# A two-layer conditioned network on one core: unread products in the first layer's TensorE pauses, the gates moved back, and the second layer's set-up with element 0's scores first

## The chip, the core and the metric

The kernel runs on one core of a Trainium2 chip. Its engines are TensorE (PE, matrix products; PEld are its weight loads), VectorE (DVE), ScalarE (ACT), GpSimd (POOL) and SyncE (SP, which here only issues transfers). The metric is the device time of one execution in microseconds (us).

## The reference

Input x is 2 batch elements of 512 tokens with 128 channels, and a condition vector of 128 per element. Two layers follow one another.

Layer 0 quantises weights to -1, 0, 1 and activations to 8 bits around every linear map:

```python
def _bitlinear(x, w, nw, b=None):
    xn = x * rsqrt(mean(x**2) + 1e-08) * nw
    xq = _act_quant(xn)            # round(xn * 127 / max|xn|), row by row
    return xq @ _weight_quant(w).T
# six parameters per element come from the condition by a small network
mx = _layernorm(x) * (1 + sc_msa) + s_msa
i, f, g = _bitlinear(mx, wi), sigmoid(_bitlinear(mx, wf)), _bitlinear(mx, wg)
o = scan over tokens: h = f * h + silu(i) * (1 - f)
x = x + g_msa * _bitlinear(_rmsnorm(o) * silu(g), wo)
x = x + g_mlp * gated MLP of (_layernorm(x) * (1 + sc_mlp) + s_mlp), 128 -> 2*512 -> 128
```

Layer 1 is plain float: `mod = silu(condition) @ Wada + bada` gives two shifts, two scales and two gates; then causal attention with 16 heads of 8 channels over 512 tokens, and a GELU MLP of 128 -> 512 -> 128, each added to x after it is multiplied by its gate.

## The kernel before

Tokens lie on the 128 partitions in 4 tiles (NT) per batch element b = 0, 1. The PSUM has 8 banks of 512 floats. Every engine has its own program, written out by hand in one order, and the engines meet only through semaphores. An instruction that waits holds all that stands behind it on its engine. There is no planner.

**Layer 0** (36 to 121 us of the profiled execution) is a chain that passes between the engines. For each element VectorE forms `mx` and three scaled copies `u3` (L1165 to L1182), GpSimd takes roots (`root`, L402), TensorE turns `u3` into columns by transposes (`to_columns`, L1538), ScalarE copies them to bf16 (`xq3`, L630), TensorE multiplies (`rows_product`, L1543), ScalarE makes sigmoids (`gate`, L648), VectorE the input of the scan, the scan itself (L1210) and the output rows. Then come the residual, the layer norm, and the MLP with its product `prod` (L1318), its scaled copy `uh` (L458), its quantisation (L1335), its columns (L1644) and its second product (L1653).

Between the pieces TensorE runs **unread products**: `idle_products(n, bk)` (L1549) issues n bf16 products of 128x512 into a bank whose content nobody reads. They stand in TensorE's order like any other instruction, each string after some wait and ahead of the next piece of work.

The **gates** of layer 1 (`layer_gates`, L1530 and L1532, four products of 128x128 and four one-row bias products, float32, into bank 7) stand after element 0's three products; ScalarE copies them to `gates` (L668) between two of its sigmoid groups, and GpSimd multiplies `Wproj`, `bproj`, `W2` and `b2` by them (L436 to L444) between the roots of stage 0 and stage 1.

**Layer 1's set-up** (119 to 147 us). `xhat` is transposed, ScalarE modulates it to `xmT` (L752), and `project_rows(b)` makes queries, keys (L1681, float32, banks 2 and 3) and values (L1687, bank 0). Queries and keys are each split in three bf16 parts: part 0 on ScalarE (L781), the rest on VectorE (L1359), part 1 on ScalarE (L789), part 2 on VectorE (L1365). The parts are stacked along the partitions in QS and KS. For element 0's first two head groups this is done by TensorE with `pick` (L1672) and copies (L768, L770, L1373); for the rest by DMAs that `stack_parts` issues, the queries on SP, the keys on GpSimd (L345, 12 per element).

Attention runs in **8 groups** n = 0 to 7 (element n // 4, four heads each). A group has 12 score items (`score_item`, L1732 to L1734, in three rotating banks); VectorE takes the negative row maximum of each (`row_maxima`, L1384). After the group's 12 items GpSimd splits the maxima in three bf16 parts (`split_maxima`, L484 to L490). TensorE transposes them after item 3 of the next group (`maxima`, L1744), ScalarE copies them (L821), SP writes them into three rows of QS (L379), and only then can the group's transposed scores, five `exp_slot`s (L1773 to L1779), begin, with the exponentials on ScalarE (L807) and the products with the values (L1793) behind them. In the kernel before TensorE's order of set-up is: element 0's projections, its picks, element 1's columns and all of its projections, then group 0. GpSimd's is: both elements' key stacks, the bias `bproj` added to xs (L476), then `split_maxima(0)`. The picks of the second group (PICK_AT) stand inside group 0.

## Time and profile before

| | |
|---|---|
| median of 3 runs | 238.95 us (237.7 to 239.03) |
| profiled execution, its own time | 238.84 us |
| its span, first to last instruction | 237.0 us |
| mean granted TensorE clock | 0.928 of full |
| busy: PE, PEld, DVE, ACT, POOL | 76%, 45%, 71%, 67%, 30% |
| chain that ended last, by engine | PE 38%, DVE 28%, ACT 14%, POOL 10%, issue 7%, DMA 1% |

The chain that ended last is followed back from the last instruction, at each step to what released it. A granted clock of 1.00 is 2.4 GHz and 0.50 is 1.2 GHz. Of the chain, the unread products of L1549 hold 5.3% of the span and the key stacks of L345 5.6%.

### The profile page before, as it was taken

Reading aid. Unit: us, or ns where it says so; the run is one execution under the profiler, and the core shown is the slowest. Engines: PE = TensorE matmul, PEld = TensorE weight load, DVE = VectorE, ACT = ScalarE, POOL = GpSimd, SP = SyncE. Lnnn points to the kernel's source line nnn. Section 1 sums busy time; section 2 is a strip of 40 time slices with the busy share of each in tenths; the row PEclk is TensorE's granted clock in tenths of the full one; section 3 lists DMA queues with packets and bytes.
Section 4 is the critical chain, followed back from the end, with each engine's and each line's share of the span. In section 5 each row is a group of like instructions: output and inputs, shape, how many; then the busy total and the mean of one; then the engine's idle time right before and its main releaser. Section 6 shows DMA issues by size and latency. Waiting matters only on the chain.

```text
span 237.0 us, 4518 instructions
## 1 busy us (share of the span) xinstructions
PE 180.2 (76%) x1640; PEld 107.6 (45%) x1644; DVE 169.1 (71%) x494; ACT 158.3 (67%) x346; POOL 71.3 (30%) x112
## 2 busy tenths in 40 slices
PE   0223369699575896559786986999999999889894
PEld 0202335676332343126453543765655665544763
DVE  3758779999688979897776694877977887342511
ACT  4798999676986866956137623765865775786141
POOL 8031231019222153971129990101110110130210
PEclk9999999776989799958999995699999999999999
DMA  5999100000000000000002340321000000000011
GB/s 140 410 427 362 52 0 0 3 1 0 0 1 0 3 0 0 1 0 0 3 1 93 97 81 23 48 53 22 3 5 2 5 3 5 2 3 0 0 47 44
DMA packets 4635, 11.50 MB, mean 49 GB/s; under 512 B 1283, under 2 KB 2788, under 8 KB 3974
## 3 DMA queue, kind: packets, MB, share of 16 engines
q1 hardware_dynamic: 3654, 10.03, 12.7%
q0 software_dynamic: 960, 1.19, 2.1%
q8 instruction: 13, 0.21, 0.4%
q14 instruction: 8, 0.07, 0.1%
HBM read 8.23 MB, written 0.52 MB: 37 GB/s over the span
## 4 chain that ended last, share of the span: by engine, by line
PE 38%; DVE 28%; ACT 14%; POOL 10%; issue 7%; DMA 1%; SPq 0%; DVEq 0%; ACTq 0%; POOLq 0%
DVE negmax L1384 7%; PE ps L1793 6%; POOL KS L345 6%; PE ps L1538 5%; PE ps L1549 5%; PE ps L1732 2%; ACT PT L807 2%; PE ps L1829 2%; DVE mx L1265 2%; PE ps L1773 2%; PE ps L1823 2%; DVE bnst L923 1%; ACT junk L623 1%; DVE amax L1308 1%; ACT xhat L594 1%
## 5 line engine op out<-in xcount | busy, mean ns | idle before, releaser
L1384 DVE TENSOR_REDUCE negmax<-ps 128x1 f32<-128x384 f32 (+3 forms) x96 | 51.2, 594 | 14.1 <-PE ps L1734 14.0
L807 ACT ACTIVATE PT<-ps 128x1024 f32<-128x1024 f32 x40 | 39.6, 1031 | 20.7 <-PE ps L1779 20.5
L1549 PE MATMUL ps<-k_b 128*128 128x512 bf16 x119 | 34.2, 449 | 6.6 <-DVE prod L1318 4.4
L1732 PE MATMUL ps<-KS,QS 48*128 48x128 bf16 (+3 forms) x128 | 32.2, 321 | 1.4 <-DVE negmax L1384 0.8
L1773 PE MATMUL ps<-QS,KS 51*128 51x512 bf16 (+3 forms) x128 | 24.9, 315 | 1.6 <-DMA QS<-nmT 1.6
L1549 PEld LDWEIGHTS ps<-k_b 128*128 128x128 bf16 x119 | 13.0, 113 | 24.7 <-issue 8.1
L1733 PE MATMUL ps<-k_b 64*128 64x128 bf16 x128 | 24.2, 229 | 0.0
L1734 PE MATMUL ps<-k_b 64*128 64x64 bf16 x128 | 21.7, 198 | 0.0
L402 POOL TENSOR_TENSOR rstd<-veps,mhalf 128x4 f32<-128x4 f32 x8 | 8.4, 1046 | 40.6 <-DVE veps L930 38.0
L1793 PE MATMUL ps<-PT,V 128*9 128x512 f32 (+3 forms) x256 | 20.4, 434 | 0.0
L402 POOL TENSOR_TENSOR rms<-vms,mhalf 128x4 f32<-128x4 f32 x10 | 10.8, 1079 | 27.5 <-DVE vms L1130 27.2
L1779 PE MATMUL ps<-k_b 64*128 64x128 bf16 x128 | 19.0, 225 | 0.0
L1776 PE MATMUL ps<-k_b 64*128 64x64 bf16 x128 | 17.9, 197 | 0.0
L484 POOL CAST nmpart<-negmax 128x16 bf16<-128x16 f32 x8 | 1.6, 199 | 52.9 <-DVE negmax L1384 52.9
L1732 PEld LDWEIGHTS ps<-KS,QS 48*128 48x128 bf16 x128 | 11.2, 96 | 10.5 <-DVE negmax L1384 7.9
L1734 PEld LDWEIGHTS ps<-k_b 64*128 64x128 bf16 x128 | 12.1, 103 | 4.4 <-issue 0.8
L345 POOL DMA_DIRECT2D KS<-part x24 | 13.4, 567 | 1.1 <-ACT part L781 0.6
L1733 PEld LDWEIGHTS ps<-k_b 64*128 64x128 bf16 x128 | 11.7, 101 | 0.0
L1773 PEld LDWEIGHTS ps<-QS,KS 51*128 51x128 bf16 x128 | 9.4, 97 | 3.7 <-issue 2.1
L1447 PE MATMUL ps<-k_f,cq 2*128 2x2 f32 x8 | 1.5, 252 | 11.6 <-DVE cq L965 11.6
L594 ACT ACTIVATE xhat<-xs,nbias,rstd 128x128 f32<-128x128 f32 x20 | 8.2, 480 | 3.1 <-DVE nbias L946 3.1
L1779 PEld LDWEIGHTS ps<-k_b 64*128 64x128 bf16 x128 | 9.2, 99 | 1.9 <-issue 0.5
(242 smaller groups left out, 452.4 us busy)
## 6 DMA issues: line engine op xcount, KB each, us to landing
w<-in_wa SPq DMA_DIRECT2D x2, 1152.0 KB, 9.4
lw<-in_l_w SPq DMA_DIRECT2D x1, 1280.0 KB
brow<-in_bcast_rows SPq DMA_DIRECT2D x1, 1152.0 KB, 15.4
mw<-in_main_w SPq DMA_DIRECT2D x1, 1024.0 KB, 12.5
KS<-part POOLq DMA_DIRECT2D x12, 64.0 KB, 3.4
QS<-part SPq DMA_DIRECT2D x12, 64.0 KB
cw<-in_cond_w SPq DMA_DIRECT2D x1, 576.0 KB, 4.0
xs<-in_x SPq DMA_DIRECT2D x1, 512.0 KB, 5.9
```

The source lines that it names most:

```text
L345: queue.dma_start(stack[first:first + HD, skip:, :], part[b][i][want][half * ROWS + skip * HD:(half + 1) * ROWS, :]).then_inc(done, 16)
L402: return nc.gpsimd.tensor_tensor(r, v, mhalf[0:v.shape[0], 0:v.shape[-1]], ALU.pow)
L807: nc.scalar.activation(PT[n % 2][:, s, :], bank(2 * (use % 2), 2), ACT.Exp).then_inc(S["p_ready"], 1)
L1384: V.tensor_reduce(negmax[n % 2][:, qt, h0:h0 + nh], bank(S_BANKS[k % 3])[:, 0:nh * w].rearrange("p (h w) -> p h w", w=w), AX.X, ALU.max, n ...
L1549: T.matmul(bank(bk).rearrange("p (r n) -> p r n", n=P), ident_b, ident_b.unsqueeze(1).to_broadcast([P, NT, P]), start=True, stop=True)
L1732: T.matmul(dst, QS[b][rows, h, tok(qt)], KS[b][rows, h, 0:w], start=True, stop=False)
L1733: T.matmul(dst[:, w - P:w], k_of("pickLo", r), k_of("maskQlo", r), start=False, stop=False)
L1734: ins = T.matmul(dst[:, w - P // 2:w], k_of("pickHi", r), k_of("maskQhi", r), start=False, stop=True)
L1773: T.matmul(dsts[half], KS[b][rows, h, tok(kt)], QS[b][rows, h, kt * P:L], start=True, stop=False)
L1776: T.matmul(dsts[half][:, 0:P // 2], k_of("pickLo", r), k_of("maskKlo", r), start=False, stop=False)
L1779: ins = T.matmul(dsts[half][:, 0:P], k_of("pickHi", r), k_of("maskKhi", r), start=False, stop=True)
L1793: ins = T.matmul(bank(PV_BANKS[n])[32 * j:32 * j + HD + 1, kt * P:L], V1[b][:, kt, g * HG + j, :], src, start=(kt == 0), stop=(kt == 2))
```

## The change

Unread products in layer 0: 11 become 19 ahead of element 0's first columns; 10 new after the shifts and 9 (were 8) after element 0's forget-gate columns; 8 new between the scanned rows of element 0 and the input columns of element 1; 3 new after each `output_columns`; at the MLP's end 16 new after the fifth product, 8 (were 10) after the last, 9 (were 6) after `uh`.

The gates: the products move from behind element 0's three products to behind `output_product(1)`, in place of 9 unread products; ScalarE's copy moves between `centre(0)` and `centre(1)`; GpSimd's eight multiplications move behind the roots of the MLP's end.

The set-up: element 1's `xhat` is made on GpSimd, not on ScalarE; element 1's projections move into groups 0 and 1 (one side after item 9, one after item 11, the values after the first item of group 1), and with them ScalarE's copies and VectorE's rests; GpSimd stacks element 0's keys, splits group 0's maxima, stacks element 1's keys, splits group 1's maxima, adds the bias.

```diff
-PICK_AT = (2, 4, 6, 8)
+PICK_AT = (3, 5, 7, 10)
+SIDE_AT = (9, 11)
@@ gpsimd
-                if stage == 0:
-                    pool.wait_ge(S["mod_copied"], 2)
-                    pool.wait_ge(S["m_q"], 4)
-                    for b in range(B):
...
             for stage in range(3, 5):
...
+            pool.wait_ge(S["mod_copied"], 2)
+            pool.wait_ge(S["m_q"], 4)
+            for b in range(B):
+                ga, gm = gates[:, 0, b, :], gates[:, 1, b, :]
+                nc.gpsimd.tensor_tensor(wproj_g[:, b, :], lw[:, slice(*LW["Wproj"])], ga, ALU.mult
+                                        ).then_inc(S["gated"], 1)
...
             pool.wait_ge(S["ln_root"], 3 * B)
+            for t in range(NT, B * NT):
+                ins = nc.gpsimd.tensor_scalar(xhat[:, t, :], xs[:, t, :], bnmv[:, t, 0:1], rstd[:, t:t + 1],
+                                              ALU.subtract, ALU.mult)
+            ins.then_inc(S["xhat_ready"], 1)
             for b in range(B):
                 nc.gpsimd.memset(V1[b][:, :, :, HD:HD + 1], 1.0).then_inc(S["v_ones"], 1)
-                pool.wait_ge(S["stack_init"], B)
-                stack_parts(pool, b, 1)
-            ...
-                nc.gpsimd.tensor_tensor(xs[:, tiles(b), :], xs[:, tiles(b), :], over_tiles(bproj_g[:, b, :]), ALU.add
+            pool.wait_ge(S["stack_init"], B)
+            stack_parts(pool, 0, 1)
             for n in range(N_GROUPS):
                 split_maxima(n)
+                if n == 0:
+                    stack_parts(pool, 1, 1)
+                if n == 1:
+                    pool.wait_ge(S["gated"], 4 * B)
+                    pool.wait_ge(S["xhat_ready"], B)
+                        nc.gpsimd.tensor_tensor(xs[:, tiles(b), :], xs[:, tiles(b), :], over_tiles(bproj_g[:, b, :]),
+                                                ALU.add).then_inc(S["biased"], 1)
@@ scalar
-            for b in range(B):
-                centre(b, B + b + 1, S["xhat_mid"])
+            centre(0, B + 1, S["xhat_mid"])
+            act.wait_ge(S["gate_pe"], 1)
+            nc.scalar.activation(gates[...], bank(7), ACT.Copy).then_inc(S["mod_copied"], 1)
+            centre(1, B + 2, S["xhat_mid"])
...
+            first_part(0, 0)
+            first_part(0, 1)
+            second_part(0, 0)
+            second_part(0, 1)
+            picked(0, 0, 0, 1, 4)
+            picked(0, 1, 0, 3, 6)
+            modulate_columns(1, 0)
+            value_rows(0)
+            picked_second(0)
+            picked_second(1)
+            picked_second(2)
+            first_part(1, 0)
+            picked_second(3)
+            first_part(1, 1)
+            value_rows(1)
...
                 copy_maxima(n - 1)
+                if n == 1:
+                    second_part(1, 0)
+                    second_part(1, 1)
@@ vector
-            ln_bias(1, 2 * B + 2)
-                    if n == 0 and i == 1:
-                        split_rest(1)
-                    if n == 0 and i == 5:
+                    if n == 0 and i == len(S_ITEMS) - 1:
+                        split_rest(1, (0,))
+                    if n == 1 and i == 1:
+                        split_rest(1, (1,))
+                    if n == 1 and i == 5:
                         split_last(1)
@@ tensor
-            idle_products(11, 2)
+            idle_products(19, 2)
...
                 if b == 0:
                     layer_shifts()
-                    layer_gates()
+                    pe.wait_ge(S["mx_ready"], 2)
+                    idle_products(10, 5)
                 pe.wait_ge(S["sig_ready"], 3 * b + 1)
                 to_columns(bank(4 * b + 2), lambda t: fg[b][:, 1, t, :], S["fT_pe"])
                 if b == 0:
-                    pe.wait_ge(S["mx_ready"], 2)
-                    idle_products(8, 5)
+                    idle_products(9, 5)
             scanned_rows(0)
+            idle_products(8, 4)
             input_columns(1)
             idle_products(8, 4)
...
             output_columns(0)
+            idle_products(3, 0)
             output_product(0)
             output_columns(1)
+            idle_products(3, 0)
             output_product(1)
-            idle_products(9, 1)
+            layer_gates()
             pe.wait_ge(S["ln_var"], B + 1)
...
+            pe.wait_ge(S["prod_ready"], B * 2 + 1)
+            idle_products(16, 0)
             pe.wait_ge(S["prod_ready"], B * NT)
-            idle_products(10, 0)
+            idle_products(8, 0)
             pe.wait_ge(S["uh_raw"], B * NT - 1)
-            idle_products(6, 0)
+            idle_products(9, 0)
...
-            project_rows(0)
+            project_side(0, 0)
+            project_side(0, 1)
+            project_values(0)
...
-            project_rows(1)
...
                     if n == 0 and i in PICK_AT:
...
+                        if v == 1:
+                            pe.wait_ge(S["xmT_ready"], B)
...
+                    if n == 0 and i in SIDE_AT:
+                        project_side(1, SIDE_AT.index(i))
+                    if n == 1 and i == 0:
+                        project_values(1)
```

## Rows read from the trace of the kernel before

**Rows 1.** Stretches of the span: busy time (instructions) by engine, granted clock, DMA share, GB/s.

```profile
47.00:50.40 3.40, 3.40 (x24) 2.70 (x21) 3.33 (x5) 3.08 (x16) 0.65 (x1) 1.00 0.00 0
50.40:57.20 6.80, 6.80 (x22) 4.14 (x22) 6.63 (x24) 3.60 (x12) 3.73 (x7) 0.50 0.00 1
...
101.60:108.40 6.80, 4.91 (x12) 1.79 (x13) 6.09 (x17) 3.76 (x10) 4.67 (x4) 0.50 0.00 0
...
142.60:152.80 10.20, 8.29 (x92) 5.70 (x92) 6.20 (x12) 5.88 (x6) 0.96 (x5) 0.50 0.26 41
173.60:182.10 8.50, 8.19 (x142) 5.17 (x137) 6.84 (x14) 5.87 (x7) 0.84 (x4) 1.00 0.01 3
```

**Rows 2.** The chain of waits, 36 to 60 us: start, duration, what.

```profile
43.32 2.75 PE ps L1538 x12
...
50.08 0.41 PE ps L1532 x2
...
52.99 3.41 PE ps L1549 x8
56.40 2.21 PE ps L1538 x16
```

**Rows 3.** VectorE in order of time, 36 to 74 us: start, duration, form, [idle before].

```profile
55.38 1.10 DVE L1198 SCALAR_TENSOR_TENSOR orow<-fg 128x512 f32<-128x512 f32 x1
...
61.37 1.13 DVE L1189 SCALAR_TENSOR_TENSOR fg<-ps,dq,fg 128x128 f32<-128x128 f32 x4 [1.44 <-ACT fg L648]
62.53 0.69 DVE L1198 SCALAR_TENSOR_TENSOR orow<-fg 128x512 f32<-128x512 f32 x1
```

**Rows 4.** TensorE in order of time, 36 to 74 us.

```profile
63.77 3.34 PE L1549 MATMUL ps<-k_b 128*128 128x512 bf16 x8
```

**Rows 5.** TensorE in order of time, 74 to 121 us.

```profile
78.32 9.53 PE L1549 MATMUL ps<-k_b 128*128 128x512 bf16 x37
88.10 2.76 PE L1549 MATMUL ps<-k_b 128*128 128x512 bf16 x12 [0.25 <-DVE mx L1125]
...
103.49 6.04 PE L1549 MATMUL ps<-k_b 128*128 128x512 bf16 x16 [4.39 <-DVE prod L1318]
...
112.75 1.05 PE L1653 MATMUL ps<-mwq,xh 128*128 128x128 bf16 x16 [0.60 <-DVE xh L1341]
```

**Rows 6.** VectorE in order of time, 74 to 121 us.

```profile
107.23 0.88 DVE L1335 TENSOR_SCALAR uh<-uh,minv 128x512 f32<-128x512 f32 x2
...
111.32 1.29 DVE L1341 TENSOR_SCALAR xh<-ps 128x512 bf16<-128x512 f32 x2 [1.54 <-PE ps L1644]
```

**Rows 7.** GpSimd by line and shape, whole span: busy, mean ns, idle before.

```profile
L440 POOL TENSOR_TENSOR w_g<-lw,gates 128x512 f32<-128x512 f32 x2 | 3.0, 1524 | 0.0
...
L407 POOL TENSOR_SCALAR cwq<-cw,whalf 128x768 bf16<-128x768 f32 x1 | 2.2, 2211 | 2.2 <-DVE cwq L1030 2.2
```

**Rows 8.** TensorE in order of time, 118 to 132 us.

```profile
126.56 1.34 PE L1672 MATMUL ps<-part,picks 128*128 128x512 bf16 x4 [1.73 <-ACT part L789]
...
129.21 1.98 PE L1681 MATMUL ps<-xmT,lw 128*128 128x512 f32 x4
131.03 1.05 PE L1687 MATMUL ps<-lw,xmT 128*128 128x128 f32 x8
```

**Rows 9.** ScalarE in order of time, 118 to 160 us.

```profile
124.34 1.65 ACT L594 ACTIVATE xhat<-xs,nbias,rstd 128x128 f32<-128x128 f32 x4 [0.62 <-DVE nbias L946]
```

**Rows 10.** VectorE in order of time, 118 to 160 us.

```profile
132.52 0.76 DVE L1384 TENSOR_REDUCE negmax<-ps 128x2 f32<-128x256 f32 x2 [2.23 <-PE ps L1734]
...
137.72 5.36 DVE L1384 TENSOR_REDUCE negmax<-ps 128x1 f32<-128x384 f32 x10
```

**Rows 11.** The chain of waits, 134 to 164 us.

```profile
139.23 2.49 POOL xs L476 x2
...
142.87 0.60 PE ps L1744 x4
...
144.89 1.89 DMA QS<-nmT
```

More of the change, by code:

```diff
@@ L711, in _ @@
             load_table(ACT.Silu, 1)
-            for b in range(B):
-                centre(b, B + b + 1, S["xhat_mid"])
+            centre(0, B + 1, S["xhat_mid"])
+            act.wait_ge(S["gate_pe"], 1)
+            nc.scalar.activation(gates[:, :, :, :].rearrange("p i b d -> p (i b d)"), bank(7), ACT.Copy
+                                 ).then_inc(S["mod_copied"], 1)
+            centre(1, B + 2, S["xhat_mid"])
             for b in range(B):
@@ L1352, in _, with split_rest @@
                     ln_apply(list(range(NT)), 2 * B + 1, S["xhat_ready"])
-            ln_bias(1, 2 * B + 2)
-            def split_rest(b):
-                for i in range(2):
+            def split_rest(b, sides=range(2)):
+                for i in sides:
                     dve.wait_ge(S["part0"], 2 * b + i + 1)
@@ L1673, in pick, with project_side, project_values @@
                                 start=(p == 0), stop=(p == 2))
-            def project_rows(b):
+            def project_side(b, i):
                 pe.wait_ge(S["xmT_ready"], b + 1)
                 a = LW[("Wqk0", "Wqkv")[b]][0]
-                for i in range(2):
-                    if b:
-                        pe.wait_ge(S["rest_ready"], i + 1)
-                    T.matmul(bank(2 + i), lw[:, a + i * D:a + (i + 1) * D], xmT[b][:, :],
-                             start=True, stop=True).then_inc(S["qk_pe"], 1)
+                if b:
+                    pe.wait_ge(S["rest_ready"], i + 1)
+                T.matmul(bank(2 + i), lw[:, a + i * D:a + (i + 1) * D], xmT[b][:, :],
+                         start=True, stop=True).then_inc(S["qk_pe"], 1)
+            def project_values(b):
                 a = LW["Wqkv"][0]
```

61 lines of the change are left out of this document (22 added, 39 removed).

## The prediction, made before the changed kernel was run

> **What bounds the kernel now.** I read the granted clock in stretches first. TensorE's clock is at 0.50 (1.2 GHz) in five separate stretches of layer 0 and again from 142.6 to 152.8 us [rows 1]; it is at 1.00 in the steady attention groups, of which one takes 8.5 us with TensorE busy 8.19 [rows 1]. Then I asked of each cold stretch whether TensorE stood on the path. The chain of waits says yes twice in layer 0: 12 transposes of 2.75 us and 8 unread products of 3.41 us, which delay 16 transposes to 56.40 [rows 2]; so do the 8 at 63.77 (3.34 us) [rows 4] and the 16 at 103.49 (6.04 us) [rows 5]. At full clock 12 take 2.76 us [rows 5], that is 0.22 each (0.23 with their end). Last, the set-up: the chain runs over GpSimd's issue of 24 key transfers, then the bias addition (2.49 us from 139.23), the split, the transposes at 142.87, and the transfer at 144.89 that lands at 146.78 [rows 11]. Groups 1 to 7 repeat behind that point, so what makes group 0 earlier should arrive at the end.
>
> **Layer 0 up to the output rows.** Eight more unread products (8 x 0.22 = 1.8 us) end near 42.9, ahead of the columns at 43.32. They cost nothing as long as the clock is full, and the 2.75 us of transposes [rows 2] shrink to about 2.0, bounded by the arrival of `u3`. VectorE has a full queue until 54 us, so this gain stays hidden. The gate instructions take 0.41 us for a pair [rows 2], 8 pairs 3.3 us, 3.9 with the slow tail; they leave, 10 unread products (2.2 us) come in. Element 0's forget columns end near 50.3, 9 products more end near 52.3, and element 1's columns start when VectorE has them, at 52.9. TensorE then waits for VectorE's `orow`, which ended at 56.48 [rows 3]. That instruction took 1.10 us against 0.69 for the same one at 62.53 [rows 3], while GpSimd multiplied by the gates; with these gone I have it at 55.95. Element 1's products then start at 56.5, where they started at 58.45 (56.40 + 2.21 of transposes less overlap [rows 2]): 2.0 us. VectorE waited 1.44 us for the sigmoids behind them [rows 3], so it follows. Next come 8 new unread products after `scanned_rows(0)` (59.7 to 61.4, the data of the next step being ready at 61.2) and the old 8, now 1.8 us in place of 3.34 [rows 4]. ScalarE's squares, picks and magnitudes run unbroken behind this, so the gain stays 2.0. **Term: -2.0.** Bounds: -2.3, and -0.5 if one of the new strings meets a cold stretch (8 products then take 3.4, 1.6 more than planned).
>
> **The moved gates.** Behind `output_product(1)` 3.3 us of gates take the place of 9 products (2.0 us). The string of 37 took 9.53 us from 78.32, of which one stretch was cold, and the next 12 waited only 0.25 us for `mx` at 88.10 [rows 5]. All warm, the new string takes 3.3 + 28 x 0.22 = 9.4 us: no loss. With one cold stretch of 3.4 us it takes 1.7 more, and of this about 0.9 reaches the next columns. The gates do not hold the clock up: from 47.0 to 50.4 TensorE was busy 3.40 of 3.40 us, mostly with them, and the clock was at 0.50 right after [rows 1]. The Trainium skill, "TensorE: Matmul & The Clock Gate", section "What's actually happening", says the gate is set by how busy TensorE has been; by that rule a stretch busy throughout keeps its clock and this term is 0, and the trace does not agree. I take **+0.4**, between 0 and +0.9. The 3 unread products after each `output_columns` (0.65 us) lie in the ScalarE copy for which TensorE waits anyway: 0. ScalarE's gate copy (0.6 us) lies in a wait for `nbias`: 0; it would cost if the gates ended later than 84.
>
> **The MLP's end.** TensorE starts 16 products at 99.7 in place of staying idle for 4.39 us [rows 5]; 16, 8 and 9 then end at 103.2, 105.2 and 107.1, before VectorE's first quantised tile at 107.67 (half of the 0.88 us at 107.23 [rows 6]). The columns of element 0 are then done near 109.45 in place of 111.3, but the copies behind them wait for ScalarE's and VectorE's quantisation of element 1 (until 110.1 and 109.8), so the second product starts at 111.3 where it started at 112.75 [rows 5]: -1.4. Against that GpSimd's gate multiplications now run from 107.8 to 113, beside this very chain. In the trace the conflict cost VectorE 0.4 us on `orow` [rows 3], and GpSimd's 512-wide multiplication took 1.52 on average [rows 7]. VectorE has about six short instructions in the way there; I take +0.6, between 0.2 and 1.5. **Term: -0.8.**
>
> The Trainium skill, "SBUF — State Buffer", section "Who interferes with whom", says that a VectorE instruction with two SBUF inputs, or in a two-port mode, and a GpSimd instruction that reads SBUF lock each other out for the whole instruction; by that rule a single meeting with the 512-wide multiplication could cost its full length and this term would be near 0.
>
> **The set-up.** GpSimd forms element 1's `xhat`: four instructions of 128x128. No such row exists; the nearest are 2.21 us for 768 columns with one input [rows 7], 0.37 for 128 by width, and the two-input ones, 1.52 for 512, 0.38 by width; so 1.5 to 1.9 us from 124.15, ending near 126. ScalarE loses its 1.65 us [rows 9] ahead of part 1, for which TensorE waited 1.73 [rows 8]. Part 1 is then there at 124.4 and 125.1, part 2 at 125.2 and 125.9 (VectorE's subtraction meets GpSimd's `xhat`: up to 0.8 later), the picks end near 126.4, VectorE's copies near 127.6. Element 1's 1.98 us of sides and 1.05 of values [rows 8] leave the space ahead of group 0. The first score starts at 127.6 to 128.4 where it started at 132.0 (0.5 before VectorE's first maximum at 132.52 [rows 10]).
> VectorE's maxima of a group take 6.4 us (the steady group's 6.84 less the divisions [rows 1]); TensorE's picks and first side stretch group 0 to 7.8 us. Group 0 is used up at 135.9; before it was 141.1 (six of the ten from 137.72 [rows 10]). GpSimd has issued 12 key transfers (6.7 us) by 133.2, so it splits at once and `nm` is ready at 137.0. Now TensorE is late: second side to 136.05, item, values 1.05, three items; the transposes start at 138.4 where they started at 142.87 [rows 11]. **Term: -4.4.** Bounds -4.9 and -3.0.
> Behind the copy of the maxima ScalarE has two new part-1 copies (1.14 us) and the table load (1.28), 2.4 us inside a wait of 2.7 for the transfer [rows 11]: 0. GpSimd's 12 key transfers of element 1 now run beside that transfer, which had the queues to itself; from 0 to +1.0, I take +0.3. `split_maxima(1)` stands behind those 12, which wait for part 2 near 142.4; they are out at 144.2, and the split is due at 145.8: 0. The bias (2.49 us) follows and has 8 us. The cold stretch after the set-up cost about 1 us (9.6 us from one copy of maxima to the next against 8.5 in the steady state [rows 1]); TensorE's thin stretch becomes 5 us in place of 9, so between 0 and -1.1 comes back, I take **-0.4**.
>
> **Sum:** -2.0 + 0.4 - 0.8 - 4.4 + 0.3 - 0.4 = -6.9. The profiled execution took 238.84 us, 0.11 under the median: 238.84 - 6.9 = 231.9.
>
> **Rivals.**
> (a) *The fills do not hold the clock where it matters*, or the strings only displace the cold stretch: the two layer-0 gains fall away and the set-up stays. 238.84 - 4.5 + 0.4 = 234.7. [...] 17%.
> (b) *The head start of group 0 turns into a wait in group 1*: element 1's rests, parts and values now stand inside the groups, and the transfer of the maxima queues among key transfers. Then only about 1.3 of the 4.4 us stay: 238.84 - 2.4 - 1.3 = 235.1. For it: TensorE is the last to arrive at the transposes; against it: VectorE stood idle 2.23 us and more there. 12%.
> (c) *Slower:* a string of unread products that runs cold becomes the path itself. The 33 at the MLP's end take 33 x 0.43 = 14.2 us at 1.2 GHz, from 99.7 to 113.9, where the columns began at 109.5: +4.4 in place of -0.8, 5.2 worse. Two cold stretches in the string of gates and 40 products cost 2.2 more, and the first gain of 2.0 goes: 231.9 + 5.2 + 2.2 + 2.0 = 241.3. It decides once such delays pass 6.9 us together. In the trace a string of 16 started cold and stayed so for 5 us [rows 1, 5]; the new one starts warm. 5%.
> The forecast itself has 66%, with a range of its own from 229.3 to 234.3.
>
> **Numbers.** Best ends of all terms: -2.3, 0, -1.2, -4.9, 0, -1.1 = -9.5, 229.3. The range goes up past (a) and (b) to 236.0. About 1% (2.4 us) is what this kernel's measurement can tell from no change, so faster ends at 236.5: the forecast, nearly all of (a) and most of (b), 0.87; same 0.07 from the worse halves of (a) and (b); slower 0.06.
>
> **What would show it.** Clock at 1.00 from 43 to 58 us and from 99 to 110; element 1's first-layer products about 2 us earlier; the second MLP product less than 1.4 us ahead of that shift; the first score about 4 us after the second layer's first picks, and no side or value product before it; the first transposes of maxima 4 to 5 us earlier on top of layer 0's shift; groups 2 to 7 unchanged at 8.5 us. A clock of 0.50 in the 33-product string, or a gap between the first maxima copy and the first `exp_slot` well over 2.8 us, would prove me wrong.

## The result, and the profile of the changed kernel

The changed kernel took **235.27 us** (median of 4 runs, 234.41 to 235.97); the kernel before, run beside it, took 238.32 us (237.28 to 239.03). The ratio is 0.988 [0.984, 0.992]: 2.9 us faster where 6.9 were forecast. The four granted clocks of the changed kernel were 0.978 to 0.985; that of the profiled execution before was 0.928, of this one 0.978. All ratios below leave out executions over 1.5% above the fastest of their kernel and medians leave out none, so the two need not agree where such executions are many (gates_xhat, gates_xhat_again).

The head of the page and the page's second part:

```profile
span 233.7 us, 4604 instructions
PE 180.8 (77%) x1685; PEld 106.0 (45%) x1685; DVE 170.7 (73%) x493; ACT 156.9 (67%) x342; POOL 74.1 (32%) x116
...
PEclk9999999999999999999799996799999999999999
```

The slices below 9 between the 8th and the 19th, which held layer 0's cold stretches (granted clock 0.50) before, are gone but for one 7 at the MLP's end; the second, at the set-up, is narrower but still there. The same in stretches (busy time by engine, granted clock, DMA share, GB/s), against [rows 1]:

```profile
50.40:57.20 6.80, 4.79 (x38) 3.06 (x35) 6.59 (x25) 4.79 (x15) 0.49 (x1) 1.00 0.00 1
99.00:105.00 6.00, 5.88 (x28) 2.41 (x26) 5.36 (x13) 3.10 (x9) 4.50 (x5) 1.00 0.00 0
111.40:114.70 3.30, 3.30 (x21) 2.77 (x19) 2.20 (x7) 0.56 (x2) 0.00 (x0) 0.52 0.00 0
141.90:148.30 6.40, 4.50 (x59) 3.35 (x61) 4.44 (x9) 2.88 (x3) 2.55 (x7) 0.50 0.68 97
```

The same points of both traces, in us from the start of the span (starts of the instruction named):

```
                                        before    after   gain
quantisation of element 1, layer 0      107.23   105.14   2.09
second product of layer 0's MLP         112.75   110.81   1.94
layer 1's first product (sides)         121.10   119.69   1.41
first score                             132.02   127.28   4.74
copy of the first group's maxima        143.48   138.77   4.71
first exponential                       147.72   144.61   3.11
copy of the second group's maxima       153.05   149.67   3.38
copy of the third group's maxima        161.42   158.11   3.31
end of the span                         237.0    233.7    3.3
```

The gain reaches 4.7 us at the set-up and shrinks twice: from 2.09 to 1.41 at the MLP's end, and from 4.71 to 3.11 between the first group's maxima and the first exponential. Groups behind that take 8.44 us each, as before. What stands at these two places:

TensorE: the strings of unread products (L1565) of layer 0's second half, the MLP's second product, and the transposes ahead of the attention, against [rows 5]:

```profile
79.34 6.22 PE L1565 MATMUL ps<-k_b 128*128 128x512 bf16 x28
...
86.01 2.76 PE L1565 MATMUL ps<-k_b 128*128 128x512 bf16 x12 [0.46 <-DVE mx L1140]
...
97.65 7.59 PE L1565 MATMUL ps<-k_b 128*128 128x512 bf16 x33 [0.65 <-DVE prod L1333]
...
110.81 1.59 PE L1674 MATMUL ps<-mwq,xh 128*128 128x128 bf16 x16 [0.97 <-DVE xh L1356]
...
126.69 0.66 PE L1554 MATMUL ps<-k_f,xhat 128*128 128x128 f32 x4 [1.25 <-POOL xhat L468]
```

VectorE at the MLP's end, against [rows 6], and under it GpSimd there and in the set-up:

```profile
105.14 1.08 DVE L1350 TENSOR_SCALAR uh<-uh,minv 128x512 f32<-128x512 f32 x2
106.15 0.41 DVE L1164 SCALAR_TENSOR_TENSOR dq<-stepq,wmean,rms 128x4 f32<-128x4 f32 x1
...
106.66 1.13 DVE L1154 SCALAR_TENSOR_TENSOR stepq<-amax,guard 128x4 f32<-128x4 f32 x1
...
109.39 1.28 DVE L1356 TENSOR_SCALAR xh<-ps 128x512 bf16<-128x512 f32 x2
```

```profile
106.50 1.27 POOL L456 TENSOR_TENSOR w_g<-lw,gates 128x512 f32<-128x512 f32 x1
...
122.88 3.75 POOL L468 TENSOR_SCALAR xhat<-xs,bnmv,rstd 128x128 f32<-128x128 f32 x4 [0.18 <-POOL rstd L403]
126.76 6.72 POOL L346 DMA_DIRECT2D KS<-part  x12
...
136.87 3.36 POOL L346 DMA_DIRECT2D KS<-part  x6
140.69 3.33 POOL L346 DMA_DIRECT2D KS<-part  x6 [0.46 <-ACT part L790]
```

The chain of waits at the second place, against [rows 11]:

```profile
138.35 0.40 PE ps L1769 x4
138.77 0.59 ACT nmT L833
...
140.18 3.49 DMA QS<-nmT
143.81 0.61 PE ps L1798 x2
```

Three things are to be seen. `stepq`, an instruction on 4 numbers per partition, took 1.13 us and ended at 107.79, when GpSimd's `w_g` ended (107.77). `xhat` on GpSimd took 3.75 us for four tiles, ended at 126.6, and TensorE waited 1.25 us for it. And the transfer of the maxima took 3.49 us where it took 1.89 [rows 11], between two series of key transfers that GpSimd issues at 136.87 and 140.69.

### The profile page after: what moved, and what is told of

Read it like the earlier page. It is cut to its first block, busy times and chain, and to the rows that moved or that the text cites. A ratio compares the mean times of both kernels' runs of the same rounds, so it can differ in the third digit from the quotient of the medians.

```text
span 233.7 us, 4604 instructions
## 1 busy us (share of the span) xinstructions
PE 180.8 (77%) x1685; PEld 106.0 (45%) x1685; DVE 170.7 (73%) x493; ACT 156.9 (67%) x342; POOL 74.1 (32%) x116
## 4 chain that ended last, share of the span: by engine, by line
DVE 36%; PE 31%; ACT 16%; issue 7%; POOL 5%; DMA 3%; SPq 1%; DVEq 0%; ACTq 0%; POOLq 0%
DVE negmax L1398 7%; PE ps L1818 6%; PE ps L1757 4%; PE ps L1554 3%; ACT PT L819 2%; PE ps L1854 2%; DVE amax L1323 2%; DVE mx L1280 2%; DMA cw<-in_cond_w 2%; ACT junk L628 2%; PE ps L1798 2%; ACT junk L513 2%; PE ps L1848 2%; DVE u L1188 2%; DVE bnst L938 2%
## 5 line engine op out<-in xcount | busy, mean ns | idle before, releaser
L1565 PE MATMUL ps<-k_b 128*128 128x512 bf16 x160 | 37.2, 382 | 3.2 <-DVE orow L1232 1.8
L1757 PE MATMUL ps<-KS,QS 48*128 48x128 bf16 (+3 forms) x128 | 30.8, 314 | 1.6 <-DVE negmax L1398 1.4
L1565 PEld LDWEIGHTS ps<-k_b 128*128 128x128 bf16 x160 | 15.3, 99 | 21.3 <-DVE orow L1232 2.3
L1758 PE MATMUL ps<-k_b 64*128 64x128 bf16 x128 | 23.2, 224 | 0.0
L1759 PE MATMUL ps<-k_b 64*128 64x64 bf16 x128 | 20.9, 195 | 0.0
L1804 PE MATMUL ps<-k_b 64*128 64x128 bf16 x128 | 19.2, 225 | 0.0
L1801 PE MATMUL ps<-k_b 64*128 64x64 bf16 x128 | 18.0, 197 | 0.0
L1757 PEld LDWEIGHTS ps<-KS,QS 48*128 48x128 bf16 x128 | 10.8, 96 | 11.6 <-DVE negmax L1398 9.0
L1759 PEld LDWEIGHTS ps<-k_b 64*128 64x128 bf16 x128 | 11.5, 100 | 4.0 <-issue 0.3
L1758 PEld LDWEIGHTS ps<-k_b 64*128 64x128 bf16 x128 | 11.4, 100 | 0.0
L443 POOL TENSOR_TENSOR uh<-prod,brow 128x512 f32<-128x512 f32 x7 | 8.7, 1264 | 4.5 <-DVE prod L1333 4.5
L1804 PEld LDWEIGHTS ps<-k_b 64*128 64x128 bf16 x128 | 9.2, 99 | 1.9 <-issue 0.5
```

The source lines that it names most:

```text
L1565: T.matmul(bank(bk).rearrange("p (r n) -> p r n", n=P), ident_b, ident_b.unsqueeze(1).to_broadcast([P, NT, P]), start=True, stop=True)
L1757: T.matmul(dst, QS[b][rows, h, tok(qt)], KS[b][rows, h, 0:w], start=True, stop=False)
L1758: T.matmul(dst[:, w - P:w], k_of("pickLo", r), k_of("maskQlo", r), start=False, stop=False)
L1759: ins = T.matmul(dst[:, w - P // 2:w], k_of("pickHi", r), k_of("maskQhi", r), start=False, stop=True)
L1801: T.matmul(dsts[half][:, 0:P // 2], k_of("pickLo", r), k_of("maskKlo", r), start=False, stop=False)
L1804: ins = T.matmul(dsts[half][:, 0:P], k_of("pickHi", r), k_of("maskKhi", r), start=False, stop=True)
```

## The experiments

All start from the changed kernel unless a text says otherwise. "after_again" is the changed kernel itself, run once more beside gates_only, gates_xhat_again and gates_xhat_fill5.

```
                     median us   ratio to before [95%]     span of the profile
keys_late               237.45   0.996 [0.993, 0.999]      236.3
gates_wait              234.98   0.986 [0.977, 0.995]      231.9
xhat_act                234.49   0.983 [0.978, 0.989]      232.6
all_three               236.18   0.993 [0.988, 0.998]      234.3
keys_split              236.32   0.993 [0.990, 0.997]      234.5
mended                  235.70   0.990 [0.986, 0.994]      235.3
setup_only              235.82   0.990 [0.986, 0.995]      233.5
fills_gates_back        235.34   0.987 [0.982, 0.993]      233.4
gates_xhat              236.55   0.983 [0.976, 0.989]      233.1
gates_xhat_thirds       238.78   0.999 [0.996, 1.003]      237.4
gates_xhat_fill         234.06   0.985 [0.980, 0.990]      231.5
no_keys1                233.67   0.980 [0.976, 0.985]      233.0
gates_only              238.03   0.997 [0.992, 1.001]      234.2
after_again             235.35   0.987 [0.982, 0.993]      234.4
gates_xhat_again        233.49   0.978 [0.972, 0.984]      231.1
gates_xhat_fill5        233.68   0.981 [0.975, 0.987]      232.2
```

**keys_late.** Element 1's key transfers are issued a group later, so that nothing runs beside the first transfer of maxima.

```diff
                 split_maxima(n)
-                if n == 0:
-                    stack_parts(pool, 1, 1)
                 if n == 1:
+                    stack_parts(pool, 1, 1)
+                if n == 2:
                     pool.wait_ge(S["gated"], 4 * B)
```

> The changed kernel with element 1's twelve key transfers issued behind the split of group 1's maxima instead of group 0's (and the bias behind group 2's). Theory (transfers queue): the copy of the first maxima (12 rows, 6 KB each half) took 3.5 us from issue to landing beside the key transfers and 1.9 without them, so the first transposed scores come 1.3 to 1.6 us earlier, the time falls by 1.0 to 1.6 us to about 0.983 of the kernel before; the transfer of group 1's maxima, now beside the keys, is hidden or gives back up to 1. Rival (the clock): the transfer time stays at 3.5 us, because it comes from something else, and nothing changes: 0.988.

The chain of waits, the first and the second transfer of maxima:

```profile
141.05 1.89 DMA QS<-nmT
...
150.59 4.18 DMA QS<-nmT
```

The first is back at 1.89 us, so the keys beside it are what made it 3.49. But the second now takes 4.18, and the third group's maxima come at 160.84 against 158.11 (0.9 us of that was there at the first copy already, behind a cold stretch at 128 to 132 us): the kernel is slower than the change.

**gates_wait.** GpSimd's gate multiplications wait for VectorE's quantised tiles.

```diff
             pool.wait_ge(S["m_q"], 4)
+            pool.wait_ge(S["uh_ready"], B * NT // 2)
             for b in range(B):
```

> The changed kernel with GpSimd's eight gate multiplications held back until VectorE has issued its four quantisations of uh (a wait on uh_ready at 4). Theory (port between VectorE and GpSimd): stepq falls from 1.13 to 0.2 us, the second element's quantisation starts 1.4 us earlier, the columns' copies end 1.5 us earlier, TensorE's pauses shrink and the clock stays at 1.00 at 111 us (0.5 us more); time 1.5 to 2.0 us less, about 0.981 of the kernel before. Rival: the multiplications only move their damage behind, to the addition to xs and to the root of the layer norm, then at most 0.5 us less, 0.986.

VectorE at the MLP's end:

```profile
105.15 0.88 DVE L1351 TENSOR_SCALAR uh<-uh,minv 128x512 f32<-128x512 f32 x2
...
106.27 0.16 DVE L1155 SCALAR_TENSOR_TENSOR stepq<-amax,guard 128x4 f32<-128x4 f32 x1
...
107.70 1.29 DVE L1357 TENSOR_SCALAR xh<-ps 128x512 bf16<-128x512 f32 x2
...
111.39 1.48 DVE L1285 TENSOR_TENSOR xs<-xs,mx 128x512 f32<-128x512 f32 x1
```

`stepq` is back from 1.13 to 0.16 us, the two tiles from 1.08 to 0.88, the copies start at 107.70 instead of 109.39, and the MLP's second product at 109.14 instead of 110.81. So the conflict cost 1.7 us up to this point of the path. TensorE's clock over 111 to 114 us was 1.00 here. Part of the conflict moved: `xs` meets the gates now and takes 1.48 in place of 0.69, so layer 1's first product, at 118.27, is only 0.9 us ahead of that of after_again (119.18). The times alone (0.986, against 0.988 for the change) would not have told: the four runs are 233.62 and 233.68 us at a granted clock of 0.984, 236.28 at 0.971 and 236.76 at 0.956.

**xhat_act.** Element 1's `xhat` goes back to ScalarE, behind element 0's part 2.

```diff
-            for t in range(NT, B * NT):
-                ins = nc.gpsimd.tensor_scalar(xhat[:, t, :], xs[:, t, :], ...
-            ins.then_inc(S["xhat_ready"], 1)
...
             second_part(0, 1)
+            centre(1, 2 * B + 1, S["xhat_ready"])
             picked(0, 0, 0, 1, 4)
...
             split_rest(0)
+            ln_bias(1, 2 * B + 2)
             split_last(0)
```

> The changed kernel with element 1's xhat made on ScalarE as before the change, but behind both part-1 copies. Theory (GpSimd's xhat is the slow piece: 0.94 us for each of four tiles, ready at 126.6, and it slows VectorE's subtractions): xhat is ready near 125.0, the first score comes about 1 us earlier, bounded by VectorE's copies of the picked keys; TensorE carries it to the first transposes of maxima; time 0.7 to 1.1 us less, 0.984. Rival (TensorE's load between the first score and the maxima is the bound and ScalarE's copies of the picked rows come later by the 1.65 us): 0 to 0.3 us less, 0.988.

ScalarE's `xhat`, and TensorE's transposes of it and the first score:

```profile
123.44 1.63 ACT L595 ACTIVATE xhat<-xs,nbias,rstd 128x128 f32<-128x128 f32 x4
```

```profile
125.12 0.66 PE L1552 MATMUL ps<-k_f,xhat 128*128 128x128 f32 x4
126.50 0.21 PE L1755 MATMUL ps<-KS,QS 48*128 48x128 bf16 x1 [0.73 <-DVE KS L1385]
```

Four tiles take 1.63 us on ScalarE against 3.75 on GpSimd, and it fits behind part 2. From layer 1's first product to the first score it is 6.97 us instead of 7.59. That 0.62 us is what GpSimd's `xhat` cost.

**all_three** has the edits of keys_late, gates_wait and xhat_act together.

> The three edits together: key transfers behind the split of group 1, GpSimd's gate multiplications behind VectorE's quantisation, element 1's xhat on ScalarE. If the three causes are separate and all on one chain the gains add: 3.2 to 4.5 us less than the changed kernel, 0.970 to 0.975 of the kernel before. If they overlap (a wait that only moves), under 2 us less, above 0.980.

First exponential at 141.93 against 144.61, 2.7 earlier; the second transfer of maxima took 4.02 us, and the third group's maxima came at 158.70, 0.6 later than in the change. What the other two edits had won was lost at the keys.

**keys_split and mended.** Element 1's key transfers in two portions, each issued once the transfer of maxima before it has landed; mended has the edits of gates_wait and xhat_act as well.

```diff
                 split_maxima(n)
-                if n == 0:
-                    stack_parts(pool, 1, 1)
-                if n == 1:
+                if n < 2:
+                    pool.wait_ge(nm_stacked[n], 32)
+                    stack_parts(pool, 1, 1, ((0,), (1, 2))[n])
+                if n == 2:
                     pool.wait_ge(S["gated"], 4 * B)
```

> The changed kernel with element 1's key transfers in two lots, six behind the landing of group 0's maxima and six behind the landing of group 1's, and the bias behind group 2's split, so that no copy of the first two maxima travels beside keys. Theory (the transfers of the maxima queue among the key transfers; with the keys moved whole the second one took 4.2 us in place of the first): both copies land 1.9 us after their issue, the first exponential starts 1.5 us earlier than in the changed kernel and nothing comes back: 1.3 to 1.6 us less, 0.982 of the kernel before. Rival (the second transfer was long because of SP's query transfers): the second stays above 3 us and the gain is lost, 0.988 or more.

> Key transfers in two lots, gate multiplications behind VectorE's quantisation, element 1's xhat on ScalarE, together. If the three causes add: 1.5 + 1.7 + 0.9 = 4.1 us less than the changed kernel, 0.971 of the kernel before, a span near 230. If one of them only moves a wait: 0.976 or more.

keys_split, the chain of waits:

```profile
140.03 1.88 DMA QS<-nmT
...
149.31 3.01 DMA QS<-nmT
...
159.01 3.35 DMA QS<-nmT
```

The wait keeps the portion off one transfer but not off the next: GpSimd issues six keys in 3.4 us after the wait (142.20 to 145.56), and 39 packets of its queue still move beside the second transfer, from 149.3 to 152.3. Now two transfers are long instead of one. In mended the second took 4.05.

**setup_only and fills_gates_back.** setup_only has layer 0 as it was before the change (fills and gates) and the new set-up of layer 1. fills_gates_back has the fills of the change and only the gates back in their old place.

```diff
+                if stage == 0:
+                    pool.wait_ge(S["mod_copied"], 2)
...
-            layer_gates()
+            idle_products(9, 1)
...
                     layer_shifts()
+                    layer_gates()
```

> The kernel before with the set-up's part of the change alone (layer 0, its fills and its gates as before). Theory: first score 3.3 us earlier, first copy of maxima 3.3 earlier, first exponential only 1.7 earlier, since the transfer between them meets the key transfers; time 1.9 us less, 0.992. Rival (the prediction's own sizes): 4.5 us less, 0.981.

> The changed kernel with all new unread products but the gates (products, ScalarE's copy, GpSimd's multiplications) where they were. Theory: the gates cost the 2.0 us that the first half of layer 0 had gained (element 1's columns start near 56), but the quantisation of uh is free of GpSimd, so the second MLP product starts about where the changed kernel has it, 110.8 to 111.5; time within 0.7 us of the changed kernel, 0.986 to 0.991. Rival (the fills alone bring the first gain): 1.5 us less than the changed kernel, 0.982.

setup_only gave 2.5 us (0.990). Its third group's maxima came at 157.90, before those of the whole change. Its layer 0 is that of the kernel before, instruction for instruction, and yet it was faster in this execution: the quantisation of element 1 starts at 106.22 against 107.23, and layer 1's first product at 119.90 against 121.10. One cold stretch of the five is missing; element 0's first columns, which took 2.75 us [rows 2], ran at full clock:

```profile
43.35 1.88 PE L1555 MATMUL ps<-k_f,u 128*128 128x128 f32 x12 [1.08 <-DVE u L1172]
```

So about 1 us of what the comparison with the profiled execution of the kernel before shows for layer 0 is the difference between two executions of the same layer 0. fills_gates_back gave 0.987, as the change does: with the new fills in place, moving the gates won nothing net. The trace shows both halves. VectorE's output rows, around 55 us, meet the gates again:

```profile
55.43 1.10 DVE L1214 SCALAR_TENSOR_TENSOR orow<-fg 128x512 f32<-128x512 f32 x1
```

The quantisation of element 1 starts at 106.90 instead of 105.14 (1.8 us lost), but with GpSimd idle at the MLP's end its second product starts at 110.88 against 110.81 in the change: the 1.7 us are back.

**gates_xhat, gates_xhat_thirds, gates_xhat_fill, no_keys1.** gates_xhat has the edits of gates_wait and xhat_act and leaves the keys as the change has them. thirds sends the keys in three portions of four, each behind a landed transfer of maxima. fill puts ten unread products in front of the first exponential slot, where TensorE waits for the transfer. no_keys1 leaves out element 1's key transfers and computes element 1's scores from what the memory holds; it shows a cost and is no version to use.

```diff
+                    if n == 1 and E_NEW.get(i) == 0:
+                        idle_products(10, 6)
                     if i in E_NEW and n >= 1:
                         exp_slot(n - 1, E_NEW[i])
```

```diff
-                if n == 0:
-                    stack_parts(pool, 1, 1)
...
-                    pe.wait_ge(k_stacked[b], 32 * len(K_PART))
+                    if b == 0:
+                        pe.wait_ge(k_stacked[b], 32 * len(K_PART))
```

> The changed kernel with the two edits that were not on the transfers: gate multiplications behind VectorE's quantisation and element 1's xhat on ScalarE; the key transfers stay where the change has them. If both causes are real and separate, the second MLP product starts near 109.1, and from the second layer's first projection to the copy of the first maxima it takes 18.5 us in place of 19.1; 1.7 + 0.6 = 2.3 us less than the changed kernel, 0.978 of the kernel before, a span near 231.4. If the clock's cold stretches take the place of what is saved: 0.984.

> The same with element 1's twelve key transfers in three lots of four, each behind the landing of the maxima of groups 0, 1 and 2. Theory (any 64 KB key transfer still under way when a copy of maxima is sent delays it): a lot of four is out in 2.3 us and landed 3.4 later, before the next copy is sent, so all copies land in 1.9 to 2.5 us; 1.0 to 1.5 us less than without this edit. Rival (SP's query transfers, which go out in the same stretches, share the queues with the keys): copies of groups 1 and 2 take 3 us or more, and it comes to the same time or up to 1.5 us more.

> The two edits of gates_xhat and ten more unread products (bank 6) in TensorE's wait for group 0's maxima, ahead of the first transposed scores. Theory of the clock: the stretch of 6 us at 0.50 that follows the wait in the changed kernel goes, TensorE feeds the exponentials at their own pace (gaps of 0.15 to 0.66 us between the first four go), from the first exponential to the second copy of maxima it takes 4.4 us in place of 5.1; 0.5 to 0.9 us less. Rival (the clock was cold already before the wait, or the transfer sets the pace): no difference within 0.3 us.

> The changed kernel without element 1's twelve key transfers (they are left out, and element 1's scores are computed from the memory as it is). It measures what they cost where the change put them. Theory: the first copy of maxima lands in 1.9 us in place of 3.5 and the rest of the trace keeps its distances, 1.4 to 1.6 us less than the changed kernel, 0.982. Rival (the length of the copy has another cause): 3.5 us as before, 0.988.

no_keys1, the first transfer of maxima in the chain, then the same of thirds, the first and the third:

```profile
141.02 1.89 DMA QS<-nmT
```

```profile
139.11 1.89 DMA QS<-nmT
...
156.91 2.02 DMA QS<-nmT
```

Without the keys the transfer takes 1.89 us, with SP's query transfers issued behind it as before: the keys are the cause. From the first to the fourth copy of maxima no_keys1 takes 26.32 us, the kernel before 26.39, the change 27.79 and after_again 27.52, so the keys cost 1.2 to 1.5 us there. With thirds the transfers of maxima in the chain are short, but the keys are late: TensorE's first score of element 1 waits for them.

```profile
164.30 0.26 PE L1764 MATMUL ps<-KS,QS 48*128 48x128 bf16 x1 [2.54 <-DMA KS<-part]
```

The clock is at 0.51 over 163.5 to 173.7, and 0.999 is left. In fill the ten products ran cold, 3.91 us from 138.78 to 142.69, about 1.1 us past the time at which the wait for the transfer ends in gates_xhat (141.6); the third group's maxima came at 155.99 against 155.53 in gates_xhat_again, so in one trace the products only cost. But the clock was at 1.00 over 144 to 147 us, and in gates_xhat it had been low for ten microseconds (busy time by engine, clock, DMA share, GB/s; first fill, then gates_xhat):

```profile
144.00:147.00 3.00, 2.60 (x52) 2.07 (x51) 3.00 (x7) 2.80 (x4) 0.77 (x4) 1.00 0.58 67
```

```profile
141.00:151.00 10.00, 9.38 (x105) 6.00 (x109) 6.29 (x12) 5.71 (x6) 4.08 (x8) 0.52 0.48 61
```

**gates_only, after_again, gates_xhat_again, gates_xhat_fill5.** gates_only is the change with the strings of unread products put back to those of before; gates_xhat_again is gates_xhat once more; the last has five products in place of ten.

```diff
-            idle_products(19, 2)
+            idle_products(11, 2)
...
-                    idle_products(10, 5)
...
-            pe.wait_ge(S["prod_ready"], B * 2 + 1)
-            idle_products(16, 0)
```

> The changed kernel with every new unread product taken away and the old strings at their old lengths; the gates (products, ScalarE's copy, GpSimd's multiplications) and the set-up stay as changed. Theory A (the gates leaving is the gain, the fills add little): element 1's columns start by 53.7 and the quantisation of uh near 105.3; at the MLP's end the 16 cold products hide GpSimd's interference, the second product starts near 111; time as the changed kernel, 0.987 to 0.991. Theory B (the fills are the gain): the quantisation of uh near 107, the second product near 112.5; 1.7 us more than the changed kernel, 0.995.

> The changed kernel itself once more, as the control for the others of this call: 0.988 of the kernel before.

> The kernel with the gate multiplications behind VectorE's quantisation and element 1's xhat on ScalarE once more, beside the control. Theory: 2.3 us less in the trace up to the copy of the first maxima and, averaged over where the clock falls, 1.0 to 2.3 us less in the time, 0.979 to 0.984. Rival (the saved time makes TensorE's pauses thin and is given back as cold stretches): no difference from the control.

> The same with five (not ten) unread products in TensorE's wait for group 0's maxima. Theory: even cold (0.43 us each, 2.1 us) they end before the copy lands, so they cost nothing, and where the clock was full they may keep it; the first scores are not late as with ten (1.1 us), 0 to 0.8 us less than without them. Rival (five leave too long a pause behind them, the clock falls all the same): no difference.

gates_only's profile looks as if the fills were worth nothing: element 1's quantisation starts at 104.95, as with them, although its 16 products started cold again.

```profile
101.22 5.17 PE L1565 MATMUL ps<-k_b 128*128 128x512 bf16 x16 [4.39 <-DVE prod L1333]
```

Its other executions say otherwise. Over its ten, granted clocks go from 0.920 to 0.956 and times from 235.99 to 239.73 us, and the profiled one was the shortest, at 0.956. The changed kernel, on the same chip, had 0.978 to 0.985 in six runs. Between the medians lie 2.7 us, between the ratios (0.987 and 0.997, whose intervals just touch) 2.2: with the gates moved, the fills keep TensorE's clock over most executions, and a single trace could not show it.

Four kernels with the new set-up now differ only in fills and gates (median us, ratio to before):

```
                      gates in their old place          gates moved
old fills             setup_only         235.82, 0.990  gates_only  238.03, 0.997
new fills             fills_gates_back   235.34, 0.987  the change  235.27, 0.988
```

The fills are worth some 2.2 to 2.7 us only where the gates have moved; with the gates in their old place they are worth 0.5 to 0.7 us, which is not clear of noise. Moving the gates without the fills costs 1.5 to 2.2. Together the two changes to layer 0 bring about 0.5 us, and by the intervals (0.986 to 0.995 against 0.984 to 0.992) it may be nothing. Why the moved gates cost so much without the fills no run shows. The four were not run side by side, so each is compared through the kernel before.

**after_again** is the same program as the change, and its trace shows what a single execution can hide:

```profile
110.83 1.05 PE L1674 MATMUL ps<-mwq,xh 128*128 128x128 bf16 x16 [0.96 <-DVE xh L1356]
```

```profile
128.00:132.00 4.00, 4.00 (x24) 1.26 (x21) 2.26 (x5) 1.23 (x3) 4.00 (x9) 0.57 0.32 100
```

The cold stretch of the change at the MLP's end (111.4 to 114.7) is absent, and layer 1's first product starts 0.5 us earlier, at 119.18. Another stands at 128 to 132 instead, and from the first score to the copy of the first maxima it takes 12.99 us in place of 11.49.

**The best version.** gates_xhat_again has the best ratio, 0.978 [0.972, 0.984] against 0.987 [0.982, 0.993] for the change beside it, and the shortest trace, though its transfer of maxima still takes 3.46 us. But the ratio flatters it. With gates_xhat, the same kernel, it has twelve executions: six of 232.93 to 234.93 us at 0.977 to 0.985, and six of 236.46 to 238.49 at 0.956 to 0.964. The median of all twelve is 235.7, no better than the change's 235.35. The two kernels with ten or five more products have twelve as well, of 232.99 to 236.44 us at 0.969 to 0.991, median 233.8. So the safer choice is gates_xhat_fill5: 233.68 us, 0.981 [0.975, 0.987], 1.7 us below the median of the change beside it (their intervals overlap) and 4.6 below the kernel before (238.25).

That its five products do anything is not shown. In its trace the clock had fallen by 139.6 us, before they began at 140.10, and stayed at 0.50 to 146; they ended before the transfer landed and cost nothing. Its median is that of gates_xhat_again (233.49), as the expectation's rival had it. In fill the clock was low as well when the ten products began, but back at 1.00 behind them. Whether the low clocks of gates_xhat are its own, cured by the products, or came from outside in just those executions, the runs do not settle.

## Why the prediction was right in direction and wrong in size

In short, three terms of the sum failed: the conflict with GpSimd at the MLP's end (taken at 0.6 us, measured 1.7), GpSimd's `xhat` in the set-up (1.5 to 1.9, measured 3.75, of which 0.6 us reach the path), and the transfer of the maxima beside the key transfers (0.3, measured 1.6). A fourth error lies under them: layer 0's gain was added up against one execution of the kernel before.

Steps against the profiled execution, in us:

```
term                                              forecast   measured
layer 0 up to the output rows, moved gates   -2.0 and +0.4     -2.09
the MLP's end                                         -0.8     +0.68
the set-up                                            -4.4     -3.30
transfer of the maxima beside the keys                +0.3     +1.60
the clock behind it                                   -0.4     -0.2
sum                                                   -6.9     -3.3
```

**Layer 0's first half** came out at its number, half of it by luck. `orow` took 0.69 us and ended at 55.97, where 55.95 was forecast. That removing the gates does this is shown by fills_gates_back (1.10 again, and the quantisation of element 1 1.8 us later). But against setup_only, whose layer 0 is the same as before the change, the gain is 1.08 us and not 2.09. And the quantisation starts at 104.95 in gates_only, without the new fills: in the traces this gain is the gates' alone. The gates' new place cost nothing on TensorE: 28 products took 6.22 us and the 12 behind them waited 0.46 us against 0.25. The clock was at 1.00 over 50.4 to 57.2, with TensorE busy 4.79 of 6.80 us. Before, it was at 0.50 there, behind a stretch busy throughout [rows 1]. By the rule of the Trainium skill, "TensorE: Matmul & The Clock Gate", section "What's actually happening", that the gate is set by how busy TensorE has been, the busier kernel should have kept its clock; the trace does not agree.

**The MLP's end** failed at one number: "I take +0.6, between 0.2 and 1.5" for the conflict between VectorE and GpSimd. gates_wait measured 1.7. The forecast counted six short instructions slightly stretched, as `orow` had been by 0.4. In fact a short instruction can stand still for the whole of a long one: 0.97 of the 1.7 us is `stepq` alone, the rest are 0.2 us on each pair of tiles and 0.2 on each `dq`. What moved from one place had to be priced at the other by the longest instruction moved, not by an average. The forecast had cited the Trainium skill, "SBUF — State Buffer", section "Who interferes with whom", by which the term would be near 0; its lock for a whole instruction is what the trace shows (1.13 us, ended with GpSimd's 1.27). The other 0.5 us came from a stretch of low clock over 111.4 to 114.7, where the second product took 1.59 us instead of 1.05. It belongs to that execution and not to the conflict: after_again has the conflict and a second product of 1.05 us. The gain that the fills were to bring here was sized right: in gates_wait the second product stands 3.61 us before that of the kernel before, 2.09 of it from the first half, so 1.5 where 1.4 was forecast. With the conflict in the way none of it is left in the traces: from the start of that quantisation to the second product it takes 5.67 us in the change and in gates_only alike.

**The set-up** was 1.1 us short. "So 1.5 to 1.9 us" for GpSimd's four `xhat` was wrong by a factor of two: 3.75 us, in the trace 0.79 for the shortest and 1.31 for the longest. The nearest rows had been taken by width from other forms of instruction [rows 7]. xhat_act puts its effect at 0.62 us. Counted from layer 1's first product the forecast had the first score after 6.5 us (127.6 less 121.10; 7.3 at its later end); it came after 7.59, and after 6.97 in xhat_act, where it waits 0.73 us for VectorE's copy of the picked keys. From the first score to the first transposes of maxima it took 11.07 us where 10.8 were forecast (138.4 less 127.6). No run takes the rest apart.

**The transfer** is the second mis-sized term: "from 0 to +1.0, I take +0.3", measured +1.6, outside its own bounds. This is what rival (b) named, "the transfer of the maxima queues among key transfers". It was given 12% and a loss of 3.1 us; the mechanism was there and cost half of that. The prediction had named the sign itself, a gap well over 2.8 us between the first copy of maxima and the first `exp_slot`: it was 4.45 us (139.36 to 143.81). The result, 235.27, is inside the range (to 236.0) but above the forecast's own (to 234.3), and next to (b)'s 235.1 by the sum of the mis-sized terms, not by (b) alone: 3.3 of the set-up's 4.4 us did reach the copy of the maxima. no_keys1 shows the cause. keys_late, keys_split, mended and thirds show that delaying the keys only passes the cost on: 4.18 us at the second transfer, 3.01 and 3.35 at the second and third, or 2.54 us of waiting for the keys themselves. From the first to the fourth copy of maxima it takes 29.53 us in keys_late, 28.77 in keys_split, 29.11 in mended and 29.64 in thirds, against 27.79 in the change.

**The clock behind it**: cold from 141.9 to 148.7 instead of 142.6 to 152.8. It gave about 0.2, counted from the copies of the second and third maxima.

**The rivals.** The condition of (a), that the fills do not hold the clock, is refuted by gates_only against after_again: they hold it (0.978 to 0.985 against 0.920 to 0.956) and are worth some 2.2 to 2.7 us there. But its outcome, that the set-up's gain stays and next to nothing comes from layer 0, is close to what the medians say: setup_only alone took 2.5 us off, the two changes to layer 0 another 0.5, where 4.5 and 2.4 were forecast. Rival (c) is refuted: the 33 products took 7.59 us, not 14.2. What stays open is the share of each term in the average execution: the kernel before had granted clocks from 0.914 (240.34 us) to 0.942 (236.75 us), so a sum made against one of its executions can be off by more than a microsecond.

## What to carry to other kernels

Work that is moved on one engine to make room is priced at its new place by its longest instruction, once for each neighbour that it can hold up there, and an instruction form without a row gets the bound, not the width-scaled guess. A small transfer on which a chain waits should be out before bulk transfers are issued; here putting the bulk later only moved the cost to the next small one. The worth of unread products is read from many executions and their granted clocks, never from one trace. A change made of parts needs a run for each part: here two parts of layer 0, worth 2 us and more against each other, were together worth about 0.5.

## What the runs showed of the hardware

- GpSimd's subtract-and-multiply with two operands per partition on 128x128 floats took 0.79 us at best, 0.94 on average and 1.31 beside VectorE's two-input subtraction (L1379), where ScalarE needs 0.41 for the same (1.63 for four).
- A VectorE instruction on 128x4 numbers took 1.13 us in place of 0.16, ending with GpSimd's 512-wide multiplication.
- The transfer of the maxima (two of 6 KB) took 1.89 us alone and 3.0 to 4.2 us with key transfers of 64 KB each about it.
- Executions of one kernel on one chip differed by 3 us with the granted clock (gates_wait: 233.62 at 0.984, 236.76 at 0.956).
- In two executions of the changed kernel a stretch of clock 0.50 lay at different places (111 to 115 us, 128 to 132 us) and delayed what stood there by 0.5 and by 1.5 us.
